# VectorE, not TensorE's identity product, adds the gathered source rows in the steps of a graph kernel that carry sorted columns

## The reference

```
h_src = h[row]
ef = concatenate([h_src, h[col]], axis=1)
edge_weights = sigmoid(relu(ef @ We1 + be1) @ We2 + be2)[:, 0]
aggr = segment_sum(edge_weights[:, None] * h_src, col, num_segments=n)
gate = sigmoid(concatenate([h, aggr], axis=-1) @ Wg + bg)
h_new = gate * aggr + (1.0 - gate) * h
```

## Time and profile before

| | |
|---|---|
| median of 3 runs | 2032.33 us (2027.09 to 2037.23) |
| the profiled execution | 2030.64 us, of which the span of its instructions is 2028.9 us |
| busy share of the span | PE 87%, DVE 77%, POOL 68%, ACT 66% |
| edge stage, first to last gather issued | 491.7 to 1929.5 us |
| steps with riders | from about 800 us on |

### The profile page before, as it was taken

How to read it: one execution, slowest core, us unless ns; L and a number is a source line. 1 busy time by engine, 2 the same in 40 slices (tenths; PEclk the granted TensorE clock), 3 DMA queues, 4 the chain that set the end, 5 groups by cost and what they waited for, 6 DMA issues and landing times.

```text
span 2028.9 us, 42803 instructions
## 1 busy us (share of the span) xinstructions
PE 1762.4 (87%) x13262; PEld 1398.9 (69%) x13263; DVE 1560.1 (77%) x4602; ACT 1338.8 (66%) x3369; POOL 1375.0 (68%) x1415
## 2 busy tenths in 40 slices
PE   3899998667687789999999999999999999989880
PEld 2787777555465556666777778878887888778750
DVE  7877887596899657777788877778877887767766
ACT  1565555475655206778888878788877887767635
POOL 4564741167677777777777777777777777777736
PEclk9999998789678859898999999999998999999985
DMA  7898998415544455666666666777666677767502
GB/s 272 278 306 289 329 313 294 154 42 197 174 130 137 142 157 166 177 178 190 189 198 193 190 209 200 208 204 215 197 209 196 198 213 212 212 188 213 148 11 64
DMA packets 293551, 395.44 MB, mean 195 GB/s; under 512 B 73153, under 2 KB 195780, under 8 KB 293195
## 3 DMA queue, kind: packets, MB, share of 16 engines
q1 hardware_dynamic: 236559, 240.51, 37.6%
q0 software_dynamic: 54144, 147.92, 25.2%
q10 hardware_dynamic: 2620, 4.25, 0.6%
HBM read 377.32 MB, written 15.17 MB: 193 GB/s over the span
## 4 chain that ended last, share of the span: by engine, by line
PE 51%; POOL 24%; issue 11%; DVE 8%; DMA 3%; DVEq 1%; SPq 1%; ACT 1%; ACTq 0%; POOLq 0%
POOL x_rows L998 14%; PE psum L531 10%; PE psum L581 6%; PE psum L565 6%; POOL late_gathers L998 5%; POOL ring L998 5%; PE psum L1494 4%; PE psum L1495 4%; PE psum L1529 4%; PE psum L1506 4%; PE psum L1382 2%; PE psum L1537 2%; PE psum L560 2%; DVE stats L1869 1%; PE psum L1412 1%
## 5 line engine op out<-in xcount | busy, mean ns | idle before, releaser
L998 POOL DMA_INDIRECT x_rows<-src_table,lane_src x680 | 656.5, 966 | 216.0 <-issue 204.7
L585 DVE TENSOR_TENSOR sums<-sums,psum 128x128 f32 (+3 forms) x822 | 207.0, 252 | 181.2 <-issue 115.1
L576 DVE TENSOR_SCALAR weighted<-iota,lane_dst,weight 128x40 f32<-128x40 f32 x1128 | 262.4, 329 | 17.3 <-ACT weight L1205 17.2
L998 POOL DMA_INDIRECT late_gathers<-src_table,lane_src x224 | 217.0, 969 | 68.3 <-issue 67.6
L998 POOL DMA_INDIRECT ring<-src_table,lane_src x224 | 215.4, 962 | 68.3 <-issue 67.6
L531 PE MATMUL psum<-ring 128*64 128x128 f32 x3128 | 225.4, 288 | 35.3 <-issue 30.2
L565 PE MATMUL psum<-x_rows,ident 128*128 128x512 f32 x340 | 198.3, 677 | 46.0 <-DMA x_rows<-src_table,lane_src 46.0
L570 DVE SCALAR_TENSOR_TENSOR psum<-psum,we_all 128x512 f32<-128x512 f32 (+1 forms) x216 | 187.0, 866 | 50.5 <-PE psum L565 50.5
L531 PEld LDWEIGHTS psum<-ring 128*64 128x64 f32 x3128 | 177.6, 142 | 60.7 <-issue 42.8
L1217 ACT ACTIVATE sums<-psum 128x512 f32<-128x512 f32 (+1 forms) x149 | 87.4, 587 | 172.7 <-PE psum L1495 172.2
L572 DVE TENSOR_REDUCE logit<-psum 128x4 f32<-128x512 f32 (+1 forms) x216 | 184.6, 855 | 16.6 <-issue 0.8
(11 more groups left out here) (266 smaller groups left out, 3887.2 us busy)
## 6 DMA issues: line engine op xcount, KB each, us to landing
ring<-in_edge_attr SPq DMA_DIRECT2D x195, 512.0 KB, 5.3
ring<-cell_table SPq DMA_DIRECT2D x145, 256.0 KB
ring<-rel_table SPq DMA_DIRECT2D x70, 512.0 KB
ring<-src_table SPq DMA_DIRECT2D x192, 128.0 KB
x_rows<-src_table,lane_src POOLq DMA_INDIRECT x680
ring<-dst_table SPq DMA_DIRECT2D x282, 32.0 KB
ring<-src_table SPq DMA_DIRECT2D x106, 64.0 KB
src_table<-ring SPq DMA_DIRECT2D x12, 512.0 KB, 2.9
```

The costliest lines, as they stand in the source:

```text
L576: last = eng.tensor_scalar(out[:, j, :], iota1[:, 0:W], dst[:, j:j + 1], wt[:, j:j + 1], ALU.is_equal, ALU.mult)
L585: return eng.tensor_tensor(table[..., bass.ds(start, width)], table[..., bass.ds(start, width)], part, ALU.add)
L998: eng.indirect_dma_start(gathered(c)[:, j, :], None, src_table, bass.IndirectOffsetOnAxis(ap=lane_src[:, t:t + 1], axis=0)).then_inc(gathe ...
```

## The change

In steps with a rider the identity product is left out, and the destination part closes the accumulation (`stop=True`). VectorE waits itself for the destination part and the gather, adds the gathered rows to the PSUM bank with one `tensor_tensor`, drains, and goes on with `edge_dots`. In steps without a rider all stays as it was; the semaphore of `hidden_sum` now counts those steps alone (`pe_adds`).

```diff
-        def dst_part(eng, out, hot_t, win):
+        def dst_part(eng, out, hot_t, win, whole=False):
             for j in range(J):
-                last = eng.matmul(out[:, j, :], hot_t[:, j, :], win, start=(j == 0), stop=False, skip_group_check=True)
+                last = eng.matmul(out[:, j, :], hot_t[:, j, :], win, start=(j == 0), stop=whole, skip_group_check=True)
             return last
...
+        vector_adds = set(q for q in riders)
+
+        def pe_adds(q):
+
+            return sum(1 for p in range(q) if p not in vector_adds)
...
-                    last = dst_part(eng, hidden(q, k), onehot3_t[:, q % T_SLOTS, k, :, :], window[0:WP, c % Q_SLOTS, :])
+                    last = dst_part(eng, hidden(q, k), onehot3_t[:, q % T_SLOTS, k, :, :], window[0:WP, c % Q_SLOTS, :], q in vector_adds)
...
             def hidden_sum(q):
+                if q in vector_adds:
+                    return
                 for k, c in enumerate(step_chunks[q]):
...
             def logits(q):
-                need(eng, "hidden_sum", q)
                 need(eng, "weight", q - 4)
+                if q in vector_adds:
+                    need(eng, "hidden", q)
+                    for k, c in enumerate(step_chunks[q]):
+                        eng.wait_ge(gather_in[c % G_SLOTS], 16 * J * (c // G_SLOTS + 1))
+                        eng.tensor_tensor(hidden(q, k), hidden(q, k), gathered(c)[:, :, 0:P], ALU.add)
+                    eng.drain()
+                else:
+                    need(eng, "hidden_sum", pe_adds(q))
                 edge_dots(eng, logit[:, q % 4, :, :].rearrange("p c j -> p (c j)")[:, 0:step_rows(q)], hidden_step(q)).then_inc(done("logit"), 1)
```

## The result

| | before | changed |
|---|---|---|
| median | 2030.33 us (2027.09 to 2037.23, 4 runs) | 2142.03 us (2131.47 to 2157.37, 4 runs) |
| ratio | 1 | 1.0548, 95% [1.0508, 1.0589] |
| profiled run, its span | 2030.64, 2028.9 us | 2137.04, 2135.3 us |

The change costs 112 us; 30 were forecast. The sign was right, the size was wrong, and the time lies above the range of 2036 to 2100 us.

What follows compares the result with a forecast made beforehand. GpSimd's gather issue was taken as the floor. VectorE's remaining waits of 58 us exceeded its room by 28 us in the stretch, 29.6 over all riders; added to 2030.64 this gave 2060 us, range 2036 to 2100.

Steps and rivals of the forecast that it cites:

- What bounds the kernel: Riders' stretch, 800 to 1900 us: GpSimd's gather issue is the floor, one per 1.26 us, with TensorE in step.
- The addition's price: VectorE, each rider step: 0.69 us for the addition plus 0.076 for the drain, 0.767 us, 109.6 us in the stretch.
- The ledger of VectorE: VectorE in the stretch: 960.6 us committed plus 109.6 added, 29.8 of 1100 us room left, 58 us of waits remaining.
- term (a): VectorE's 97 waits behind the sigmoid, 122.6 us, shrink to 22 us as TensorE's products come earlier.
- Term (b): TensorE's 19.3 us of waiting for gathers moves to VectorE and is kept whole.
- TensorE's lead of 1.05 us comes off each: Rider steps: products come 1.05 us earlier, cutting each 1.26 us VectorE wait behind the sigmoid to 0.21 us.
- Rival C: TensorE's granted clock falls in the riders' stretch, deciding below 0.80; at 0.75, 75 us more, 2106 us; chance 0.13.
- B: No change: VectorE's room of 29.8 us is enough and gathers remain the only bound, 2031 us; chance 0.15.
- D: Faster: TensorE is the bound and the gathers' pace loosens with it, 17 us won, 2014 us; chance 0.04.
- the sign of C: Profile, 800 to 1900 us: VectorE still idles before the rider's one-hots while the granted clock is below 0.85.
- GpSimd's tens of us of waiting: Sign in the stretch: GpSimd waits tens of us for `wsum` instead of 2.1, as slower VectorE reaches the gathers.
- TensorE's share: Sign in the stretch, 800 to 1900 us: TensorE's busy share down to 83 to 88%.

Runs made afterwards that it cites:

- e12: Kernel before with all TensorE products kept, plus an addition of zeros and a drain on VectorE in each rider step: 2056.08 us, 1.0131.
- e16: Changed kernel without VectorE's addition, with a same-size product on node-table rows in the identity product's old place: 2029.53 us, 0.9979.
- e15: Changed kernel, VectorE's addition kept, with a same-size product on node-table rows in the identity product's old place: 2055.78 us, 1.0117.
- e6: Changed kernel without VectorE's addition, so neither product nor addition in rider steps; TensorE waits for the gather: 2092.09 us, 1.0311.
- e11: Changed kernel without VectorE's addition, plus an unused identity product before the rider's dots in each rider step: 2053.96 us, 1.0111.
- e5: The changed kernel itself, unedited, timed again beside the kernel before: 2138.71 us, 1.0584.
- e13: Changed kernel, VectorE's addition kept, plus an unused identity product before the rider's dots in each rider step: 2105.95 us, 1.0364.
- e17: Changed kernel without VectorE's addition, four one-column matmuls in the identity product's old place: 2676.95 us, 1.0243, kernel before at 2611.62.
- e2: Changed kernel without VectorE's addition, so neither product nor addition in rider steps: 2602.52 us, 1.0082, kernel before at 2583.23.
- e14: Changed kernel with VectorE adding in every second rider step only, TensorE's product kept in the others: 2070.53 us, 1.0189.
- e9: Changed kernel without VectorE's addition, plus an unused identity product before the rider's dots: 2588.91 us, 1.0029, kernel before at 2584.43.
- e4: Kernel before with all TensorE products, plus VectorE's addition of zeros and drain in rider steps: 2588.33 us, 1.0023, kernel before at 2583.23.

## Why the prediction was wrong

**What bounds the kernel: right on the average, and too coarse.** Over the stretch GpSimd's issue is the floor, and no version came below it. But a rider step of the kernel before takes 6.2 us, more than the 5.05 of its four gathers, and TensorE is busy in it throughout; the steps without a rider make up for that, with some 4 us for two chunks (where one follows a rider step, the dots lie 10.2 us apart in the median). In rider steps there was no room for slower products.

**The addition's price: right.** 0.704 and 0.083 us, 0.787 instead of 0.767 a step.

**The ledger of VectorE: near in size, and partly by luck.** It says 29.6 us; the load alone costs 26.7 (e12), or 26.3 (e16 to e15). But it let term (a) shrink from 122.6 to 22 us by TensorE's lead. In e12 there is no lead, and the same waits shrink to 42.6 us (39.3 before the one-hots, 3.3 before 576), because a later VectorE waits less. A part of the 26.7 is the clock as well: 15 of e12's 104 rider steps have a part at the lower clock and take 8.5 us on average, against 12 of 106 and 8.0 before. How large that part is isn't shown. Term (b), 19.3 us for gathers waited for on VectorE, was argued to be kept whole: e15 has that wait on VectorE and e12 on TensorE, and they measure 1.0117 and 1.0131, so on which of the two engines the wait stands makes no difference that can be told.

**The step that failed: "TensorE's lead of 1.05 us comes off each".** The removal of the product was costed as a gain for VectorE (term (a)) and otherwise at nothing, since TensorE isn't the floor. The working never asked what the identity product hid. It hid `rider_relu`: TensorE has 1.31 us of work between the rider's products and its dots, and ScalarE needs about 0.9 us of it (1187.01 to 1187.93 in the chain of e6). Without the product TensorE stands there, 36 us in the changed kernel and 49 in e6 where it was 1. That hole isn't what costs: at the full clock the rider steps are no longer with it (6.17 and 6.10 us against 6.22). It does use up the gain, so even at the full clock there is no lead to hand on. What costs is that without the product the granted clock falls from 0.96 to 0.87 over the stretch, and the products get longer (394 to 445 ns). TensorE's time per gather stays at 1.24 us although a seventh of its work (153 of 1069 us) was taken away. The 1.05 us never reach VectorE: its idle time before the one-hots is 105.0 us where it was 106.5, while e12, with the product, brings it to 39.3. In e6, without the addition, it even rises to 174.5 us (line 2021 there, in 800:1900):

```profile
  issue: 166.0, 79
  ACT weight L1215: 8.5, 4
```

That the clock is the cause and not a companion: adding a wide product brings clock and time back, in three pairs (e6 to e11, 0.86 to 0.95 and 40 us; e5 to e13, 0.87 to 0.95 and 2.2 points; e5 to e15, 0.87 to 0.95 and 90 us). Within one execution the gathers keep their full pace where the clock is 0.97. And the rider steps that have the full clock are as short as ever; the time is in those that don't. So the 69 us are the clock, and the lost cover costs nothing by itself at a full clock. What these runs don't separate is by what the missing product brings the clock down: by the holes, or by there being less work in the same time. The thin products (e17) fill time without doing the work and bring neither clock nor time back, but they were timed only where the kernel before takes over 2600 us, and the holes there were not measured. It also stays open why a lower clock costs so little in those groups: in e2 it falls to 0.76 from 0.80 over the whole execution, as far as in e6 (0.86 from 0.91), and the time rises by 0.8% instead of 3.1%.

**Rival C was the right mechanism with a wrong point of decision.** It was put "below 0.80", from TensorE's total of 916 us filling 1100. The clock fell to 0.87 only, and the missing product alone cost 69 us, nearly the 75 that C gave for a clock of 0.75. The total over the stretch was the wrong measure: the lower clock falls on single rider steps, which take 10.42 us where it holds throughout, twice the 5.05 of their gathers, and the steps at the full clock have no spare time to make it up. TensorE needn't be busy 100% over a stretch for that: in the slow stretches of 100 us it is busy for 91 to 95%.

"TensorE: Matmul & The Clock Gate" of the Trainium skill was weighed in the prediction (throttled by default, released by activity), with a chance of 0.13 for the rival behind it; the traces agree in so far as TensorE got less clock when it had less to do (0.96 before, 0.86 in e6). Its section "A second HAM failure mode: psum-queue depth-cycling" comes nearer still. It tells of another kernel: a TensorE that idles briefly between groups of matmuls, its instructions at full speed in the median, loses throughput to a clock that goes up and down. Here the holes are 0.54 us each (36.2 us in 67), and the changed kernel's clock is 0.80 in one 100 us and 0.97 in another.

**Rivals B and D.** B falls with e12: VectorE's room isn't enough even when nothing else is changed. D falls too: in e6, where nothing but TensorE's product is gone, no 100 us of the stretch have more than 80 gathers, and e16 issues 870 in the 1100 us, as the kernel before (872). In the full-clock steps of e6 TensorE is idle for a part and the step is as long as before.

**What would have shown it.** The prediction named the sign of C, VectorE idle before the one-hots at a clock "below 0.85". The idle time is there; the clock over the riders is 0.87, and 0.80 in the stretch from 1200. GpSimd's tens of us of waiting are there as well, but it was to come with a full VectorE (92% or more), which is at 80%. TensorE's share was to be 83 to 88%, and is 90.6%: the sign that its work had become longer. Half of the steps changed (e14) cost 38 us, a third of the whole: the price grows faster than the number of steps changed.

No version here beats the kernel before beyond the 0.5%; in the riders' stretch GpSimd has only 2.1 us of waiting to give.

## What to carry to other kernels

Before work is taken off an engine that isn't the bound, look at what stands directly behind it and what that waits for: work that "costs nothing" may be the cover for another engine's latency. Where TensorE is one of several engines in a loop and its granted clock is near 1, don't take that clock for given when a large product goes: cost the removal also at the lower level that the trace already shows, and per step, not over a whole stage. Two runs take such a change apart: the new load alone with the product kept, and the product gone without the load; here they gave 27 and 65 us. And when a clock and a time fall together, compare single steps at the same clock: that told the price of the hole from the price of the clock.

## What was not expected of the hardware

Useless work on TensorE made the kernel faster: one product of 1.07 us a rider step, 90 us over the kernel (e5 to e15).

With matmuls of one column TensorE was busy for 1360 of 1500 us at a clock of 0.70 (e17), with a product of 512 columns in another place of the step for 1279 us at 0.80 (e9).

Where the kernel before takes 2583 us or more (one chip gave this and, in another group, 2033), the profiles of the edited kernels have a wait that is not there at 2030 us. From the waits of e4 in 900:2400, and its timeline at 1507 us:

```profile
ACT sums L1223 <- remote: 291.7, 65, 7.8
```

```profile
1507.09 0.59 PE L1501 MATMUL psum<-sums,ring 128*128 128x256 f32 x2
...
1509.96 0.60 ACT L1223 ACTIVATE sums<-psum 128x512 f32<-128x512 f32 x1 [2.24 <-remote]
```

`rider_relu` starts 2.28 us after the end of the product that it waits for, and the profile names no instruction of this core for it. What delays it isn't known; it wasn't tried.
